# Four inverse deviations through a ScalarE square root, the first cross products in two banks, the third tile's result on VectorE

## What is computed

```python
x = _layernorm(x + attention(x))                     # 16 heads of width 8, rotary tables, softmax
x = _layernorm(x + cross(x, ctx_1024))               # circular correlation, top 11 lags, softmax, roll, projection
x = _layernorm(x + mixture_of_8_experts(x)) ...      # gates of the 2 best, gamma and beta, then a last layernorm

def _layernorm(x, axis=-1, eps=1e-05):
    m = jnp.mean(x, axis=axis, keepdims=True)
    v = jnp.var(x, axis=axis, keepdims=True)
    return (x - m) / jnp.sqrt(v + eps)
```

## Time and profile before

| | us |
|---|---|
| median of 3 runs (lowest, highest) | 239.36 (239.25, 239.49) |
| the profiled execution's own time | 238.96 |
| its span, first to last instruction | 237.2 |
| granted TensorE clock, mean share of full speed | 0.985 |

### The profile page before, as it was taken

How to read it: one execution, slowest core, us unless ns; L and a number is a source line. 1 busy time by engine, 2 the same in 40 slices (tenths; PEclk the granted TensorE clock), 3 DMA queues, 4 the chain that set the end, 5 groups by cost and what they waited for, 6 DMA issues and landing times.

```text
span 237.2 us, 7191 instructions
## 1 busy us (share of the span) xinstructions
PE 215.7 (91%) x2720; PEld 184.2 (78%) x2720; DVE 182.4 (77%) x622; ACT 133.9 (56%) x221; POOL 117.2 (49%) x231
## 2 busy tenths in 40 slices
PE   7889999999999987888899999999999999999920
PEld 6767678877786665677787999789988999789920
DVE  1689999989998998465754678986889778956871
ACT  2688989999999985421479202971059400890000
POOL 5099997989998893243820400251004400221785
PEclk9999999999999999999999999999999999999995
DMA  5930543656557652200000000010000100000001
GB/s 154 276 88 12 105 66 67 142 120 131 126 112 122 136 107 65 39 5 1 0 3 0 3 0 1 0 47 0 4 0 0 46 3 1 0 22 25 0 12 33
DMA packets 32452, 12.29 MB, mean 52 GB/s; under 512 B 19906, under 2 KB 32290, under 8 KB 32418
## 3 DMA queue, kind: packets, MB, share of 16 engines
q1 hardware_dynamic: 31698, 11.54, 22.7%
q10 hardware_dynamic: 720, 0.30, 0.5%
HBM read 6.33 MB, written 1.05 MB: 31 GB/s over the span
## 4 chain that ended last, share of the span: by engine, by line
PE 68%; POOL 11%; DVE 10%; issue 7%; ACT 2%; POOLq 0%; DVEq 0%
PE score_pair L1233 12%; PE bank L1247 11%; PE scoreT_pair L1247 11%; PE scoreT_pair L1233 7%; PE bank L983 5%; PE bank L987 4%; DVE rowmax L1299 4%; PE bank L908 3%; PE scoreT_pair L940 3%; PE score_pair L924 2%; PE bank L946 2%; POOL rs L594 2%; POOL rs L479 2%; POOL x_all L585 2%; POOL w_part L504 1%
## 5 line engine op out<-in xcount | busy, mean ns | idle before, releaser
L592 POOL TENSOR_TENSOR ve<-mv,table 128x4 f32<-128x4 f32 (+2 forms) x19 | 4.7, 246 | 79.7 <-DVE mv L1652 61.1
L1299 DVE TENSOR_REDUCE rowmax<-score_pair 128x8 f32<-128x1024 f32 x32 | 38.9, 1215 | 3.0 <-PE score_pair L924 2.0
L726 ACT ACTIVATE early<-scoreT_pair 128x1024 f32<-128x1024 f32 x32 | 32.8, 1024 | 5.2 <-PE scoreT_pair L940 4.9
L1233 PE MATMUL score_pair<-x2T_part,w_part 128*128 128x512 f32 x120 | 32.0, 402 | 0.6 <-ACT x2T_part L845 0.6
L858 ACT ACTIVATE early<-score_pair,b 128x512 f32<-128x512 f32 x40 | 27.5, 688 | 4.8 <-PE score_pair L1233 4.4
L1247 PE MATMUL bank<-w,early 128*128 128x128 f32 x256 | 30.1, 276 | 0.0
L1247 PE MATMUL scoreT_pair<-w,early 128*128 128x128 f32 x256 | 29.9, 275 | 0.0
L1247 PEld LDWEIGHTS bank<-w,early 128*128 128x128 f32 x256 | 29.5, 192 | 0.3
L1247 PEld LDWEIGHTS scoreT_pair<-w,early 128*128 128x128 f32 x256 | 29.2, 192 | 0.0
L1233 PEld LDWEIGHTS score_pair<-x2T_part,w_part 128*128 128x128 f32 x120 | 21.7, 188 | 6.6 <-ACT early L858 1.4
L983 PE MATMUL bank<-early,v_pad 128*32 128x128 f32 x512 | 26.4, 278 | 0.1
(11 more groups left out here) (204 smaller groups left out, 458.5 us busy)
## 6 DMA issues: line engine op xcount, KB each, us to landing
w<-in_w SPq DMA_DIRECT2D x8, 256.0 KB, 3.4
x_ext<-in_x SPq DMA_DIRECT2D x4, 256.0 KB, 6.1
qT_all<-mT SPq DMA_DIRECT2D x32, 32.0 KB, 2.3
early<-in_xT SPq DMA_DIRECT2D x3, 256.0 KB, 4.7
early<-in_ctxT SPq DMA_DIRECT2D x3, 256.0 KB, 5.3
out<-qkv_all SPq DMA_DIRECT2D x3, 256.0 KB, 2.3
table<-in_tables SPq DMA_DIRECT2D x1, 321.0 KB
out<-qkv_all SPq DMA_DIRECT2D x4, 64.0 KB, 1.5
```

The source lines that it names most:

```text
L726: act.activation(prob[n % 2][:, 2 * u:2 * u + 2, :, :], scoreT_pair[:, :].rearrange("p (i j s) -> p i j s", i=2, j=QUAD), ACT.Exp, scale=S ...
L1233: mm = pe.matmul(hidden_bank[c][:, :], w1_part[:, w, c * P:(c + 1) * P], x2T_part[:, x, :], start=(k == 0), stop=(k == 2))
L1299: dve.tensor_reduce(rowmax[:, H // 2 * u:H // 2 * (u + 1)], score_pair[:, :].rearrange("p (r t) -> p r t", t=S), AX_X, ALU.max).then_inc(s ...
```

## The change

Four inverse deviations are made in another way: norm 1 of tile 15, norm 2 of group 0 (in two halves), norms 3 and 4 of the last tile. ACT takes Sqrt(variance + eps) into `sd`, eps being its bias operand, and DVE takes the reciprocal. Sqrt is in another function table than Exp, so that ACT's table has to be changed. `function_table` does an activation of one column into `warm` whose result nobody reads; a load of the table is put ahead of it. There are five such places. With that, DVE writes the last tile of norm 1 in two pieces, query columns first; the cross products of tiles 0 and 1 go into `turn_bank` with a semaphore of their own; and the result of tile 2 moves from POOL to DVE, between the last statistics and tile 3's result. POOL loses its part of the four, and its `rows4(2)` now stands ahead of `last_result(1)`.

```diff
+        first_cross_bank = (turn_bank, bank[0])
...
+                elif g == G - 1 and tiles.start == GT - 2:
+                    sp.wait_ge(s["third_res"], 1)
... POOL
-            inverse_deviation(15)
...
-                if g == 0:
-                    for half in range(2):
-                        tiles = slice(HALF * half, HALF * (half + 1))
-                        rsqrt(half, tiles.stop, tiles, "y2_aggr", mv2, ve2, "ve2_ready", rs2, "rs2_ready")
-                else:
-                    rsqrt(g + 1, GT * (g + 1), ALL, "y2_aggr", mv2, ve2, "ve2_ready", rs2, "rs2_ready")
+                if g > 0:
+                    rsqrt(g - 1, GT * (g + 1), ALL, "y2_aggr", mv2, ve2, "ve2_ready", rs2, "rs2_ready")
...
             rows4(1)
+            rows4(2)
             last_result(1)
-            rows3(3)
-            rows4(2)
-            last_result(2)
-            rows4(3)
... ACT
+            def function_table(i, function):
+                act.activation(warm[:, i:i + 1], eps, function)
...
             softmax_exp(15, 1)
+            function_table(0, ACT.Sqrt)
             key_spectrum()
...
+            act.wait_ge(s["y1_aggr"], B)
+            act.activation(sd[:, 0:1], mv1[(B - 1) % DEEP][:, 1:2], ACT.Sqrt, bias=eps).then_inc(s["last_sd1"], 1)
+            function_table(1, ACT.Exp)
...
+            function_table(2, ACT.Sqrt)
...
+            def first_deviation(half):
+                tiles = slice(HALF * half, HALF * (half + 1))
+                act.wait_ge(s["y2_aggr"], tiles.stop)
+                act.activation(sd[:, 1 + HALF * half:1 + HALF * (half + 1)], mv2[:, tiles, 1], ACT.Sqrt, bias=eps)\
+                    .then_inc(s["first_sd2"], 1)
...
-            for g in range(1, G):
-                keep_x_out(g)
+            keep_x_out(1)
+            first_deviation(0)
+            keep_x_out(2)
+            first_deviation(1)
+            keep_x_out(3)
             first_pre(0)
             first_pre(1)
+            function_table(3, ACT.Exp)
...
+            function_table(4, ACT.Sqrt)
+            act.wait_ge(s["y3_aggr"], B)
+            act.activation(sd[:, 3:4], mv3[:, GT - 1, 1:2], ACT.Sqrt, bias=eps).then_inc(s["last_sd"], 1)
+            act.wait_ge(s["z_aggr"], B)
+            act.activation(sd[:, 4:5], mv4[:, GT - 1, 1:2], ACT.Sqrt, bias=eps).then_inc(s["last_sd"], 1)
... PE
-            for g in range(G):
+            for half in range(2):
+                for n in range(HALF * half, HALF * (half + 1)):
+                    mm = pe.matmul(first_cross_bank[half][:, n * D:(n + 1) * D], ...)
+                mm.then_inc(s["x_out"] if half else s["first_x_out"], 1)
+            for g in range(1, G):
                 cross_out(g)
... DVE
-            normal_rows(dve, 15)
+            dve.wait_ge(s["last_sd1"], 1)
+            dve.reciprocal(rs1[(B - 1) % DEEP][:, :], sd[:, 0:1]).then_inc(s["last_rs1"], 1)
+            dve.wait_ge(s["last_rs1"], 1)
+            for columns in (slice(D, D + XC), slice(0, D)):
+                dve.tensor_scalar(x1_all[:, B - 1, columns], ...).then_inc(s["x1_ready"], 1)
...
                 for half in range(2):
+                    dve.wait_ge(s["x_out"] if half else s["first_x_out"], 1)
...
-                    dve.wait_ge(s["rs2_ready"], half + 1)
+                    dve.wait_ge(s["first_sd2"], half + 1)
+                    dve.reciprocal(rs2[:, tiles], sd[:, 1 + HALF * half:1 + HALF * (half + 1)]).then_inc(s["first_rs2"], 1)
+                    dve.wait_ge(s["first_rs2"], half + 1)
...
```

More of the change, by code:

```diff
@@ L185, in build_program @@
         ve2 = sb("ve2", [P, GT])
+        sd = sb("sd", [P, 5])
+        warm = sb("warm", [P, 6])
         rs2 = sb("rs2", [P, GT])
@@ L230, in build_program @@
             y3_stats y3_aggr ve3_ready rs3_ready yn_ready z_ready z_stats z_aggr ve4_ready rs4_ready
-            res_ready""".split()
+            res_ready last_sd1 last_rs1 first_sd2 first_rs2 third_res last_sd last_rs first_x_out""".split()
         s = {n: sem(n) for n in names}
@@ L742, in key_spectrum @@
                 act.activation(kf[:, 1, 1, :], spectrum[:, 0, :], ACT.Copy, scale=-1.0).then_inc(s["kf_ready"], 1)
+            eps = tab("eps")[:, 0:1]
+            def function_table(i, function):
+                act.activation(warm[:, i:i + 1], eps, function)
             keep_qkv(0)
@@ L1268, in body @@
                 tail(g, more)
-            for g in range(G):
+            pe.wait_ge(s["vx_ready"], 1)
+            for half in range(2):
+                for n in range(HALF * half, HALF * (half + 1)):
+                    mm = pe.matmul(first_cross_bank[half][:, n * D:(n + 1) * D],
+                                   vx[:, 0, n, :, :].rearrange("p r c -> p (r c)"), mix[:, :], start=True, stop=True)
+                mm.then_inc(s["x_out"] if half else s["first_x_out"], 1)
+            for g in range(1, G):
                 cross_out(g)
@@ L1460, in _ @@
             normal_rows(dve, 14)
-            normal_rows(dve, 15)
+            dve.wait_ge(s["last_sd1"], 1)
+            dve.reciprocal(rs1[(B - 1) % DEEP][:, :], sd[:, 0:1]).then_inc(s["last_rs1"], 1)
+            dve.wait_ge(s["last_rs1"], 1)
+            for columns in (slice(D, D + XC), slice(0, D)):
+                dve.tensor_scalar(x1_all[:, B - 1, columns], y1[(B - 1) % DEEP][:, columns], mv1[(B - 1) % DEEP][:, 0:1],
+                                  rs1[(B - 1) % DEEP][:, :], ALU.subtract, ALU.mult).then_inc(s["x1_ready"], 1)
             dve.wait_ge(s["late_w"], 16 * n_late)
@@ L1530, in first_sums @@
                 dve.wait_ge(s["x1b_ready"], 1)
-                dve.wait_ge(s["x_out"], 1)
-                crossed = bank[0].rearrange("p (n d) -> p n d", n=GT)
                 for half in range(2):
+                    dve.wait_ge(s["x_out"] if half else s["first_x_out"], 1)
+                    crossed = first_cross_bank[half].rearrange("p (n d) -> p n d", n=GT)
                     tiles = slice(HALF * half, HALF * (half + 1))
@@ L1558, in pre_rows @@
             def pre_rows(g):
-                dve.wait_ge(s["rs2_ready"], g + 2)
+                dve.wait_ge(s["rs2_ready"], g)
                 wait(dve, s["x2b_ready"], g)
@@ L1720, in last_row @@
                                          ALU.subtract, ALU.mult).then_inc(s["yn_ready"], 1)
-                dve.wait_ge(s["rs3_ready"], G + n)
+                dve.wait_ge(s["last_sd"], 1)
+                dve.reciprocal(rs3[:, n:n + 1], sd[:, 3:4]).then_inc(s["last_rs"], 1)
+                dve.wait_ge(s["last_rs"], 1)
                 dve.wait_ge(s["yn_ready"], done + 1)
@@ L1729, in last_row @@
                 dve.bn_aggr(mv4[:, n, :], st4[:, n, :]).then_inc(s["z_aggr"], 1)
-                dve.wait_ge(s["rs4_ready"], G + n)
+                dve.wait_ge(s["rs4_ready"], G + n - 1)
+                dve.tensor_scalar(res[:, G - 1, n - 1, :], z[:, n - 1, :], mv4[:, n - 1, 0:1], rs4[:, n - 1:n],
+                                  ALU.subtract, ALU.mult).then_inc(s["third_res"], 1)
+                dve.wait_ge(s["last_sd"], 2)
+                dve.reciprocal(rs4[:, n:n + 1], sd[:, 4:5]).then_inc(s["last_rs"], 1)
+                dve.wait_ge(s["last_rs"], 2)
                 dve.tensor_scalar(res[:, G - 1, n, :], z[:, n, :], mv4[:, n, 0:1], rs4[:, n:n + 1],
```

## The result

| | before | changed |
|---|---|---|
| median of 15 runs (lowest, highest), us | 239.45 (238.85, 240.67) | 236.91 (236.35, 238.78) |
| profiled execution's own time, span | 238.96, 237.2 | 236.77, 234.8 |
| granted clock | 0.985 | 0.992 |

The ratio of changed to before is 0.9896, with a 95% interval of 0.9878 to 0.9913: 2.5 us faster (2.1 to 2.9). The forecast was 236.5, 2.88 faster, in a range of 235.9 to 237.8. In every ratio here a run more than 1.5% above the fastest of its kernel is left out as slow; the medians keep it.

The account below looks back on a forecast made before the run. TensorE held 68% of the chain, GpSimd, where the change works, 11%. Gains 0.44 + 0.47 + 1.97 = 2.88 us, taken from a median of 239.36, gave 236.5 us, range 235.9 to 237.8.

Parts of the forecast that it names:

- A: Norm 1 of tile 15: square root on ScalarE and query columns written first gain 0.44 us, ends 0.2 and 0.6.
- a first piece under 0.2: Sign in the next profile at norm 1 of tile 15: the query columns' write takes under 0.2 us.
- The square root, 0.29: Price taken for a ScalarE square root of one or two columns: 0.29 us, ends 0.15 and 0.40.
- B: Norm 2 of group 0: split products and square roots bring the first `hidden` 0.47 us sooner, ends 0.2 and 0.6.
- TensorE doesn't give it all back: Group 0's norm 2: VectorE gains 0.6 us, but first transposes stay behind products and four clock matmuls; 0.47 arrives.
- Table changes 1, 2 and 4: Loads at tile 15's norm 1, behind the lags' exponential and behind the last ReLU: cost nothing at 1.28 us each.
- Table change 3: Load ahead of the first ReLU, only one near the path: covered with 0.27 us to spare, up to 1.55 long.
- Rival 1: Each load holds ScalarE longer than its 1.28 us row, up to 3.20: time 237.2 to 238.5 us; chance 0.17.
- The bound of 2.8: At tile 15's norm 1, a load with what it drags behind it costs time only beyond 2.8 us.
- C: The end, last tile's norms 3 and 4 and the stores: gain 1.97 us, ends 1.5 and 2.1.
- rival 2: At the end, last store lands 0.6 to 0.8 us later than reckoned: gain 1.2 to 1.4, time 237.2; chance 0.07.
- Rival 3: A mid-program load takes far longer than at the start: whole gain gone at 3.6 us, slower beyond; chance 0.03.

Follow-up runs that it names:

- no_b: Changed kernel with group 0's norm 2 undone: cross products in one bank, GpSimd's power, two table changes gone; 237.20 us, ratio 0.9889 to before.
- both: Changed kernel without the four clock matmuls ahead of the first transposes, last store on ScalarE's queue; 236.12 us, ratio 0.9840 to before.
- three_loads: Changed kernel with three table changes in a row instead of one ahead of the first ReLU; 242.22 us, ratio 1.0039 to before.
- no_warm: Changed kernel without the five columns that only call for a table, so loads come on demand; 240.03 us, ratio 1.0001 to before.

## Why the prediction was right

The measured time lies in the range, and the sign is right. By its own steps, against the two traces:

- **A, 0.44**: 0.44 measured, and that is luck: two errors cancel. The handovers are shorter than I took them: VectorE to ScalarE 0.04, not 0.10, and a wait for VectorE's own reciprocal 0.04, not 0.10. The write of the 8 query columns takes 0.29, not 0.17: a write of 8 columns is hardly shorter than one of 136 (0.35), so cutting the row in two gave 0.06 instead of 0.18. The short rows I leaned on were of another kind (an aggregate, one column times a constant). The sign "a first piece under 0.2" failed for that reason.
- **The square root, 0.29**: 0.29 to 0.30.
- **B, 0.47**: 0.49 (0.48 in `no_b`). The step "TensorE doesn't give it all back" carried it: transposes at 4.68 behind `mix` in both kernels. What the text let pass is that the same floor makes the split banks worthless.
- **Table changes 1, 2 and 4, nothing**: right, all three are over before their users come.
- **Table change 3, covered with 0.27 to spare**: the first ReLU ends at 119.53, the third chunk starts at 119.87, so 0.34.
- **Rival 1** (a load holds ScalarE for longer than its row) is out: the activation behind a load starts as it ends, 118.73 behind 117.44 + 1.28, and so in every load behind the program's start in these profiles but one, whose square root had to wait for VectorE. The Trainium skill has in "ScalarE: Activation LUTs", What ACT_TABLE_LOAD costs, 1283 ns and a drain of about 1380 ns. The first figure is the trace's. Of the second nothing shows, neither ahead of a load nor behind it, in idle and in busy stretches (61 loads, the next activation 0.01 us behind each), and the measurement decides. The bound of 2.8 that the text gives for a load at A is 2.7 by its own terms, which moves only the far ends of rivals 1 and 3, by 0.1.
- **C, 1.97**: 1.88. The last result came 2.31 sooner instead of 2.14, again by shorter handovers. The last store doesn't follow the last result, though, but GpSimd's result of tile 1 and three issues in a row. These stand 0.39 and 0.48 apart, not 0.34, which is rival 2's direction at about a quarter of its price: the last issue begins 0.35 behind its result instead of 0.19. GpSimd's result in turn came 0.19 sooner than I had it. To the issue's start the gain is 1.98, so the 1.97 is hit by two errors that cancel once more; to its end it is 1.88, because the issue itself takes 0.43 us and not 0.33.
- **Rival 3** (a load in mid-program takes far longer) is out with 1.28 in all places.

The terms come to 0.44 + 0.49 + 1.88 = 2.81 of the 2.88 forecast; medians say 2.54 and the interval 2.1 to 2.9. Between the two spans, 2.4 apart, the missing 0.4 is the first column: in the changed kernel's profile the first tile's matmul pair, which both kernels have, takes 0.3 us longer, and the small one behind it 0.43 instead of 0.28.

```profile
4.18 1.18 PE L902 MATMUL bank<-wqkv,early 128*128 128x384 f32 x2
```

```profile
4.18 1.49 PE L926 MATMUL bank<-wqkv,early 128*128 128x384 f32 x2
```

(The timeline of before, and of the changed kernel.) The start moves from execution to execution by more than A or B is worth. Across the profiles the small matmuls of these first microseconds stand at two lengths, here in the kernel before and in `both`:

```profile
5.74 0.39 PE L906 MATMUL bank<-wqkv,early 128*128 128x8 f32 x2 [0.26 <-DVE wqkv L1356]
```

```profile
6.16 0.60 PE L932 MATMUL bank<-wqkv,early 128*128 128x8 f32 x2 [0.26 <-DVE wqkv L1386]
```

The trace's record of the granted clock has its first entry, 1.00, at 4.9 us in the profile of before, at 5.8 in the changed kernel's and at 10.3 in that of `both`, and the four kernels with a first entry at 9.9 us or later are the four with the latest first column (104.88 to 105.39). So TensorE's clock seems to come up later in some executions; that is argued from the order and not shown, since the record has nothing ahead of that entry. Whether the changed kernel draws the late start more often than the one before I can't tell from one profile each; that part of the 0.3 us between stages and medians stays open.

## What to carry to other kernels

A function table can be changed for nothing where its engine idles, if something asks for it there: one column of the wanted function, issued early. On demand the same loads ate the whole gain. Look for the floor beside a wait before splitting it finer (here four matmuls that kept the clock up, on TensorE's own queue), and try the last store on a queue where nothing stands ahead of it (0.25 us by the trace, not shown by the time). Before an operation moves to another engine, see what stood ahead of it in the list of the old one: another order may give part of the gain. When effects are smaller than the spread of the start, compare stages between two named instructions, not times.

## What the runs showed of the hardware that I had not expected

In the profiled execution of `three_loads` TensorE's granted clock fell to 0.50 around a wait of 2.58 us, with TensorE busy ahead of it, and was back some 6 us behind the wait's end; the stall cost 2.7 us and the lower clock 2.8 us more. In two of that kernel's twelve runs the mean clock (0.991, 0.992) shows no such fall. A wait of 0.99 us (`no_warm`, ahead of its clock matmuls) left it at 1.00, and filling the long wait with 22 unused passes kept it there too. A write of 8 columns on VectorE took 0.29 us where 136 took 0.35. And three output stores in a row on one queue were issued 0.39 and 0.48 us apart, where one alone takes 0.34.
